# Layer epilogues by groups: GpSimd centres and squares, roots by parts, and the second half of the pair products first

## The chip, the cores and the metric

The kernel runs on one core of one Trainium2 chip. The metric is device time in microseconds (us), the median of several runs. Five engines work side by side: TensorE (PE, its weight loads listed as PEld), VectorE (DVE), ScalarE (ACT), GpSimd (POOL) and SyncE (SP, which here only issues DMAs). Each has its own instruction stream; they wait for one another through semaphores.

## The reference: four graph layers, each followed by a layer norm

There are 6250 nodes with 64 features and 200000 edges. Cut to what matters here:

```python
x = layernorm(x + relu((D^-1/2 A D^-1/2 x) @ W + b))             # layer 0
x = layernorm(x + relu(x @ U.T + segment_sum(x[src], dst) @ V.T))  # layer 1
x = layernorm(x + (concat([mean_agg(x), x]) @ W.T + b))            # layer 2
# layer 3: for each edge
h = relu(concat([x[src], x[dst]]) @ W1 + b1)
i = h @ W2 + b2
g = i * sigmoid(i @ Wg + bg)
x = layernorm(x + segment_sum(g, src) / max(count(src), 1))
# layernorm(x) = (x - mean) / sqrt(var + 1e-5), over the 64 features
```

## The kernel before, in words

The nodes lie in 49 tiles of 128 rows, padded to `NTP` = 50; `X`, `AGG` and `T1` are [128, 50, 64] fp32 in SBUF. Most passes over them go by groups of 8 tiles (512 elements a partition): `EG` = 7 groups, the last with 2 tiles (128 elements).

The program first sorts the edges, then builds the dense adjacency matrix in DRAM, then runs layers 0 to 2. Each of these streams the adjacency rows in (SP's queue) and multiplies them on TensorE into an accumulator that fills seven PSUM banks. Behind that comes the **epilogue** of the layer: VectorE copies the accumulator to `AGG`, TensorE transposes it (and `X`) group by group, ScalarE copies the transposes to SBUF, TensorE multiplies by the weights, and VectorE adds the residual (`out`), takes the mean, centres, squares and sums the squares (`centre`), all of a group before the next one. After the last group it takes `variance` of all 50 tiles in one instruction, ScalarE takes one root, VectorE one reciprocal (`inverse_root`), and then it normalises group 0 and splits it into three bf16 parts (`split`) that the next layer's accumulation starts from.

After layer 2 all groups are normalised, then transposed and multiplied by the two halves of W1 (`turn_pairs`, `pair_product`). The products with the first half (A rows) stay in SBUF, split in three bf16 parts in `x3`; those with the second half (B rows) go to `AGG` and from there to a table in DRAM, `b_table`.

Layer 3 then goes over 440 *items*, each a part of one of 391 groups of 512 edges (padded to 392 groups). For each group GpSimd issues four indirect DMAs (gathers) that fetch the B rows of its 4 x 128 edges into one of `RING` = 8 slots (`gather_group`). TensorE, ScalarE and VectorE work an item through `hidden`, `interact`, `gate`, `gated` and `sum_edges`. The sequencer of GpSimd tells the others that a group has landed:

```python
if not first or s >= GLAG:                 # GLAG = 2: the group two back
    e.wait_ge(b_landed[(s - GLAG) % RING], 16 * G * (rnd + (s >= GLAG)))
    e.sem_inc(groups_landed, 1)
```

The start of the gathers hangs on `table_out` (the whole of `b_table` stored); the start of the items on `a_split` (the A rows split, `total` cleared). At the end VectorE divides `total` by the counts, adds, centres, squares and normalises, at full width, and SP stores the output in two parts.

All order is written out by hand: each engine's stream is what the code says, and the waits are on the numbers in `mark`. Line numbers in the rows below are those of this kernel: L800 to L805 `out`, L729 to L733 `centre`, L740 the reciprocal, L743 `normalise`, L717 to L721 `split`, L1444 the accumulation, L1512 the pair products, L976 the copy of the gather's indices, L994 the gathers.

## Time and profile before

| | us |
|---|---|
| median of 3 runs | 4379.18 (4379.10 to 4385.17) |
| the profiled execution, its own time | 4377.39 |
| its span in the trace | 4375.7 |
| PE busy | 3589.0 (82%) |
| DVE busy | 2414.6 (55%) |
| ACT busy | 1724.7 (39%) |
| POOL busy | 1570.6 (36%) |

The span is the profiled execution from its first to its last instruction; 1.7 us lie around it. The busy time of an engine is a mean over stages that have little in common: POOL is idle for most of the first 2329 us and busy without a break in the last stage. Times in the rows count from the start of the span.

### The profile page before, as it was taken

What the parts mean: (1) busy time and instruction counts of PE and PEld (TensorE: products, weight loads), DVE (VectorE), ACT (ScalarE), POOL (GpSimd) and SP (SyncE); (2) the same over time, 40 slices, a digit from 0 to 9 for tenths busy, and PEclk for the clock granted to TensorE, in tenths of its full rate; (3) what the DMA queues carried; (4) which work ended last, traced back from release to release, by engine and by line L of the source; (5) the groups of instructions that cost most, each with busy time, mean ns of one, the idle gap of its engine ahead of it and who ended that gap; (6) DMA issues with size and microseconds to landing.
All of it is one profiled execution on the core that took longest, in us unless ns stands there. A gap on an engine that the chain in (4) does not pass through costs nothing.

```text
span 4375.7 us, 127467 instructions
## 1 busy us (share of the span) xinstructions
PE 3589.0 (82%) x39375; PEld 2793.3 (64%) x39376; DVE 2414.6 (55%) x6572; ACT 1724.7 (39%) x3798; POOL 1570.6 (36%) x1730
## 2 busy tenths in 40 slices
PE   5784247777777798898996999889999999999886
PEld 2342123333333598897985877777877777878775
DVE  8988879999999702305024434433434343343344
ACT  5773037777777400001002434333333333343332
POOL 2000010000000000000005777777777777777773
PEclk9896579998888899999996979998889888788996
DMA  1000012222222597796962222222222222222222
GB/s 43 3 4 1 19 61 88 88 97 94 88 88 103 194 349 293 276 349 229 343 244 49 57 51 59 56 55 55 56 54 57 54 56 56 54 57 55 56 55 37
DMA packets 186859, 446.38 MB, mean 102 GB/s; under 512 B 52907, under 2 KB 115379, under 8 KB 180271
## 3 DMA queue, kind: packets, MB, share of 16 engines
q1 hardware_dynamic: 133263, 388.80, 25.6%
q0 software_dynamic: 51328, 54.71, 6.1%
q10 hardware_dynamic: 2208, 2.10, 0.2%
q8 instruction: 34, 0.56, 0.1%
q14 instruction: 26, 0.21, 0.0%
HBM read 357.45 MB, written 87.99 MB: 102 GB/s over the span
## 4 chain that ended last, share of the span: by engine, by line
PE 50%; DVE 19%; issue 10%; DMA 9%; POOL 7%; ACT 3%; ACTq 1%; POOLq 1%; DVEq 1%; SPq 0%; PEldq 0%
PE ps L1444 11%; DVE x L509 9%; PE ps L1419 8%; PE ps L1539 8%; PE ps L1529 7%; PE ps L1551 7%; PE ps L1526 6%; POOL x L994 6%; DMA rows<-adjacency 4%; DMA x<-b_table,gidx 4%; DVE rows L707 4%; ACT stage L1193 1%; PE ps L1326 1%; ACT ps L1174 1%; POOLq L988 1%
## 5 line engine op out<-in xcount | busy, mean ns | idle before, releaser
L994 POOL DMA_INDIRECT x<-b_table,gidx x1568 | 1500.1, 957 | 464.0 <-issue 375.7
L1419 PE MATMUL ps<-rows 128*128 128x448 bf16 x2272 | 650.3, 425 | 222.1 <-DVE rows L707 96.6
L1444 PE MATMUL ps<-x,rows 128*128 x22050 | 684.5, 194 | 57.3 <-DVEq L757 29.4
L1444 PEld LDWEIGHTS ps<-x,rows 128*128 128x128 bf16 x22050 | 667.2, 98 | 75.3 <-issue 65.9
L707 DVE TENSOR_SCALAR rows<-iota_c,x 128x448 bf16<-128x448 bf16 x2272 | 711.0, 408 | 2.3 <-PE ps L1419 2.3
L855 DVE TENSOR_TENSOR x<-x,ps 128x256 f32<-128x256 f32 x440 | 185.3, 421 | 945.2 <-ACT x L1260 942.3
L1419 PEld LDWEIGHTS ps<-rows 128*128 128x128 bf16 x2272 | 332.1, 146 | 540.0 <-issue 422.0
L1539 PE MATMUL ps<-w2cat,x 65*128 65x128 f32 x3520 | 575.4, 313 | 0.0
L1529 PEld LDWEIGHTS ps<-ident,x 128*64 128x64 f32 x3520 | 486.9, 157 | 106.6 <-issue 42.9
L1551 PE MATMUL ps<-x 128*128 128x65 f32 x3520 | 503.7, 291 | 49.2 <-DVE x L855 48.4
L1539 PEld LDWEIGHTS ps<-w2cat,x 65*128 65x128 f32 x3520 | 485.0, 214 | 89.2 <-issue 87.7
L1529 PE MATMUL ps<-ident,x 128*64 128x128 f32 x3520 | 539.6, 305 | 0.0
L1551 PEld LDWEIGHTS ps<-x 128*128 128x128 f32 x3520 | 486.2, 214 | 60.1 <-DVE x L855 59.5
L1526 PE MATMUL ps<-x 128*64 128x512 bf16 x1320 | 424.7, 436 | 115.8 <-issue 83.0
L1254 ACT ACTIVATE x<-ps,b1col 64x512 f32<-64x512 f32 x440 | 299.2, 680 | 486.9 <-PE ps L1529 484.5
L1247 ACT ACTIVATE x<-x 128x256 f32 x442 | 184.0, 416 | 735.7 <-POOLq L982 561.8
L1193 ACT ACTIVATE stage<-ps 128x448 bf16<-128x448 f32 x700 | 386.1, 552 | 217.1 <-PE ps L1419 207.5
L509 DVE TENSOR_TENSOR x<-x 128x512 f32<-128x512 f32 (+1 forms) x516 | 401.6, 835 | 5.6
L847 DVE TENSOR_SCALAR x<-iota_f,stage 128x128 f32<-128x128 f32 x1760 | 398.3, 304 | 0.1
L1174 ACT ACTIVATE ps<-zero_col 128x448 f32<-128x448 f32 x707 | 390.8, 562 | 0.1
L780 DVE MEMSET AGG<- 128x64 f32 x3 | 0.3, 112 | 613.3 <-PEq L1450 613.3
L965 POOL DMA_INDIRECT T<-key_rows,item_group x4 | 3.8, 942 | 917.7 <-DVE x L760 916.8
(280 smaller groups left out, 2490.3 us busy)
## 6 DMA issues: line engine op xcount, KB each, us to landing
rows<-adjacency SPq DMA_DIRECT2D x150, 800.0 KB, 6.2
rows<-adjacency SPq DMA_DIRECT2D x150, 768.0 KB, 6.0
adjacency<-stage SPq DMA_DIRECT2D x50, 1568.0 KB, 5.1
x<-src_rows SPq DMA_DIRECT2D x440, 128.0 KB
x<-b_table,gidx POOLq DMA_INDIRECT x1568
key_rows<-x ACTq DMA_DIRECT2D x1, 1024.0 KB, 4.1
pair_rows<-x ACTq DMA_DIRECT2D x1, 1024.0 KB, 7.3
pair_rows<-x SPq DMA_DIRECT2D x1, 1024.0 KB, 5.4
```

Of the source, the lines that this page charges most:

```text
L509: ins = e.tensor_tensor(view(b, high, down), view(a, 0, down), view(a, 1, down), op)
L707: ins = e.tensor_scalar(hot_dst[:, k, :], iota_c[:], rel_col[:, bass.ds(i0 + k, 1)], digit_col[:, bass.ds(i0 + k, 1)], ALU.is_equal, ALU.mult)
L847: ins = e.tensor_scalar(OS[:, s, j, :], iota_f[:], src_items[:, bass.ds(G * i + j, 1)], None, ALU.is_equal)
L994: e.indirect_dma_start(out=BGT[:, s, j, :], out_offset=None, in_=b_table, in_offset=bass.IndirectOffsetOnAxis(ap=gidx[:, s * G + j:s * G + ...
L1174: e.activation(ps[:, bank, 0:WIN], repeat(zero_col[:], WIN), ACT.Copy).then_inc(evicted, 1)
L1193: e.activation(stage[:, h, v * WIN:(v + 1) * WIN], ps[:, v % RINGW, 0:WIN], ACT.Copy).then_inc(strip_out, 1)
L1419: e.matmul(psf[:, bass.ds(at_bank, WIN)], hot_src[:, k // HOTS, :, k % HOTS], hot_dst[:, k % HOTS, :], start=False, stop=False, skip_group ...
L1444: ins = e.matmul(acc_ps[:, t, :], rows[:, h, c:c + P], x3[:, bass.ds(2 * pr + h // 2, 1), k * D:(k + 1) * D] .rearrange("p a f -> p (a f)" ...
L1526: e.matmul(ps[0:D, u, :], AT[:, s, k * D:(k + 1) * D], OT[:, u, :], start=(k == 0), stop=False, skip_group_check=True)
L1529: ins = e.matmul(ps[0:D, u, j * P:(j + 1) * P], BT[:, s, j * D:(j + 1) * D], ident[:], start=False, stop=(j == G - 1), skip_group_check=True)
L1539: ins = e.matmul(ps[:, 2 + u, j * P:(j + 1) * P], H[0:D + 1, u, j * P:(j + 1) * P], w2cat[:], start=True, stop=True)
L1551: ins = e.matmul(ps[:, 4 + u, 0:D + 1], OS[:, s, j, :], MG[:, u, j, :], start=(j == 0), stop=(j == G - 1))
```

## The change

Six edits, all in what stands between the big stages and in the last one's gathers:

1. `centre` is cut in three. VectorE sums the rows and scales the mean (`sum_rows`); GpSimd adds the mean and squares, in two `tensor_tensor` a group; VectorE sums the squares of the group two back (`sum_squares`).
2. `variance`, root and reciprocal go by two parts, tiles 0 to 31 and 32 to 49 (`ROOT`), in layers 0, 1 and the last norm, and by groups in layer 2. The second part's sums stand behind the split of group 0.
3. In layer 2 the pair products start from centred, not normalised rows; each row of the product is multiplied by its inverse root as it leaves PSUM. B products stand in the layer's own loop (`b_products`, `b_rows`), A products behind it. The bias of layer 2 is added to `X` into `T1` while the accumulation runs.
4. `b_table` is stored in three parts, each as soon as its groups are there. Clearing `total` and scaling `X` by the inverse roots goes to ScalarE (50 small instructions); the A rows are split group by group.
5. `GLAG` is 1 instead of 2, and the wait for the group before stands between the second and the third gather of a group instead of ahead of the first.
6. The last norm goes by groups, with GpSimd's share as in 1, and the output is cut at tile 32 instead of 25.

```diff
+            def sum_rows(layer, g):
+                t0, t1 = group_tiles(g)
+                mean = stat[:, 0, t0:t1]
+                e.wait_ge(dve, q.n)
+                q.link(e.tensor_reduce(mean, X[:, t0:t1, :], AX_X, ALU.add))
+                q.mark(f"mean{layer}_{g}", e.tensor_scalar(mean, mean, -1.0 / D, None, ALU.mult))
+            def sum_squares(layer, g):
+                t0, t1 = group_tiles(g)
+                e.wait_ge(centred, 2 * (layer * EG + g) + 2)
+                q.done(e.tensor_reduce(stat[:, 1, t0:t1], T1[:, t0:t1, :], AX_X, ALU.add))
...
-                    centre(t0, t1)
-                mark[f"var{layer}"] = variance()
+                    sum_rows(layer, g)
+                    if layer < 2:
+                        if g >= 2:
+                            sum_squares(layer, g - 2)
+                        if g == EG - 2:
+                            variance(f"var{layer}_0", 0, ROOT[1])
+                    else:
+                        if g >= 2:
+                            sum_squares(2, g - 2)
+                            variance(f"var2_{g - 2}", *group_tiles(g - 2))
+                        if g >= 3:
+                            b_rows(g - 3)
+            for g in (EG - 2, EG - 1):
+                sum_squares(2, g)
+                variance(f"var2_{g}", *group_tiles(g))
+                b_rows(g - 2)
+            b_rows(EG - 2)
+            b_rows(EG - 1)
...
+                def b_rows(g):
+                    t0, t1 = group_tiles(g)
+                    inverse_root(5 + g, t0, t1)
+                    e.wait_ge(pair_product, g + 1)
+                    q.mark(f"p_{g}", e.tensor_tensor(
+                        AGG[:, t0:t1, :], ps[:, 6 + g % 2, 0:(t1 - t0) * D].rearrange("p (t f) -> p t f", f=D),
+                        over_f(stat[:, 0, t0:t1]), ALU.mult))
...
+            def centre(layer, g):
+                n = layer * EG + g
+                t0, t1 = 8 * g, min(8 * g + 8, NTP)
+                xs = X[:, t0:t1, :]
+                e.wait_ge(dve, mark[f"mean{layer}_{g}"])
+                e.tensor_tensor(xs, xs, over_f(stat[:, 0, t0:t1]), ALU.add).then_inc(centred, 1)
+                e.wait_ge(centred, 2 * n + 1)
+                e.tensor_tensor(T1[:, t0:t1, :], xs, xs, ALU.mult).then_inc(centred, 1)
...
-                if not first or s >= GLAG:
-                    e.wait_ge(b_landed[(s - GLAG) % RING], 16 * G * (rnd + (s >= GLAG)))
-                    e.sem_inc(groups_landed, 1)
...
                 for j in range(G):
+                    if j == 2 and (not first or s >= GLAG):
+                        e.wait_ge(b_landed[(s - GLAG) % RING], 16 * G * (rnd + (s >= GLAG)))
+                        e.sem_inc(groups_landed, 1)
...
+                def b_products(g):
+                    e.wait_ge(pairT_copied, g + 1)
+                    if g >= 2:
+                        e.wait_ge(dve, mark[f"p_{g - 2}"])
+                    else:
+                        e.wait_ge(item_copied, ITEM_BLOCKS)
+                    pair_products(g, 6 + g % 2, 1)
```

The first place is VectorE's epilogue of layer 0, from the first group on. Before (L729 to L733 are `centre`):

```order
L800 TENSOR_TENSOR T<-ps,bias 128x512 [waits product]
L802 SCALAR_TENSOR_TENSOR X<-T,X 128x512 [waits dve]
L729 TENSOR_REDUCE stat<-X 128x8 [waits dve]
L730 TENSOR_SCALAR stat<-stat 128x8 [waits dve]
L731 TENSOR_TENSOR X<-X,stat 128x512 [waits dve]
L732 TENSOR_TENSOR T<-X 128x512 [waits dve]
L733 TENSOR_REDUCE stat<-T 128x8 [waits dve]
```

The same engine and layer in the changed kernel, the third group (g = 2), where L744 sums the squares of group 0:

```order
L826 TENSOR_TENSOR T<-ps,bias 128x512 [waits product]
L828 SCALAR_TENSOR_TENSOR X<-T,X 128x512 [waits dve]
L738 TENSOR_REDUCE stat<-X 128x8 [waits dve]
L739 TENSOR_SCALAR stat<-stat 128x8 [waits dve]
L744 TENSOR_REDUCE stat<-T 128x8 [waits centred]
```

Two of a group's seven instructions have gone from VectorE, and the last sum waits for GpSimd's second instruction of the group two back.

The second place is the end of layer 2's epilogue on VectorE in the changed kernel, from the small last group on; L814 is the multiplication in `b_rows`:

```order
L833 TENSOR_TENSOR X<-ps,T 128x128 [waits product]
L738 TENSOR_REDUCE stat<-X 128x2 [waits dve]
L739 TENSOR_SCALAR stat<-stat 128x2 [waits dve]
L744 TENSOR_REDUCE stat<-T 128x8 [waits centred]
L748 TENSOR_SCALAR stat<-stat 128x8 [waits dve]
L752 RECIPROCAL stat<-stat 128x8 [waits root_ready]
L814 TENSOR_TENSOR AGG<-ps,stat 128x512 [waits pair_product,dve]
L744 TENSOR_REDUCE stat<-T 128x8 [waits centred]
L748 TENSOR_SCALAR stat<-stat 128x8 [waits dve]
L752 RECIPROCAL stat<-stat 128x8 [waits root_ready]
L814 TENSOR_TENSOR AGG<-ps,stat 128x512 [waits pair_product,dve]
```

The first L814 here is `b_rows(3)` of the loop's g = 6, the second is `b_rows(3)` again, from g = 5 of the loop behind it: the group's rows are written twice.

The third place is GpSimd's loop of gathers, one group. Before (L988 loads a number that the group's wait for a free slot needs; `b_landed1` belongs to the group two back):

```order
L988 ISA [waits b_landed1]
L988 TENSOR_LOAD last_use
L988 ISA x2
L994 DMA x<-b_table,gidx 128x64 [waits b_copied]
L994 DMA x<-b_table,gidx 128x64 x3
```

And one group of the changed kernel, where `b_landed1` belongs to the group just before:

```order
L1043 ISA
L1043 TENSOR_LOAD last_use
L1043 ISA x2
L1052 DMA x<-b_table,gidx 128x64 [waits b_copied]
L1052 DMA x<-b_table,gidx 128x64
L1052 DMA x<-b_table,gidx 128x64 [waits b_landed1]
L1052 DMA x<-b_table,gidx 128x64
```

The wait for a landing has moved from the head of a group to its middle, and from the group two back to the one before: two gathers stand between the awaited group's last one and the wait, where there were four.

## Rows read from the trace of the kernel before

**Rows 1.** Page, costliest groups: line, engine, op, count | busy, mean ns | idle before.
```profile
L994 POOL DMA_INDIRECT x<-b_table,gidx x1568 | 1500.1, 957 | 464.0 <-issue 375.7
```

**Rows 2.** Timeline of POOL, 2264 to 2385 us: start, us, op, count [idle before <-releaser].
```profile
2329.20 1.93 POOL L976 COPY gidx<-dst_pad 128x16 int32<-128x16 int32 x2 [815.26 <-DMA b_table<-AGG]
2331.28 5.31 POOL L994 DMA_INDIRECT x<-b_table,gidx  x1
2336.89 5.08 POOL L994 DMA_INDIRECT x<-b_table,gidx  x1 [0.30 <-issue]
```

**Rows 3.** Timeline of DVE, 1724 to 1775 us (epilogue of layer 0).
```profile
1730.63 0.69 DVE L800 TENSOR_TENSOR T<-ps,bias 128x512 f32<-128x512 f32 x1 [0.58 <-PE ps L1489]
...
1732.08 0.69 DVE L729 TENSOR_REDUCE stat<-X 128x8 f32<-128x512 f32 x1
...
1733.01 0.69 DVE L731 TENSOR_TENSOR X<-X,stat 128x512 f32<-128x512 f32 x1
...
1757.93 0.29 DVE L800 TENSOR_TENSOR T<-ps,bias 128x128 f32<-128x128 f32 x1
...
1761.94 0.47 DVE L740 RECIPROCAL stat<-stat 128x50 f32<-128x50 f32 x1 [1.67 <-ACT stat L1227]
1762.44 0.69 DVE L743 TENSOR_TENSOR X<-X,stat 128x512 f32<-128x512 f32 x1
...
1765.54 0.43 DVE L721 CAST x<-AGG 128x512 bf16<-128x512 f32 x1
```

**Rows 4.** Timeline of PE: accumulation starts again, layers 1 and 2.
```profile
1766.31 8.87 PE L1444 MATMUL ps<-x,rows 128*128 x248 [15.14 <-DVEq L757]
...
2035.41 8.77 PE L1444 MATMUL ps<-x,rows 128*128 x236 [14.23 <-DVEq L757]
```

**Rows 5.** Timeline of PE, 1996 to 2044 us: transposes of two groups of layer 1.
```profile
2004.16 0.60 PE L1463 MATMUL ps<-ident,AGG 128*128 128x128 f32 x4
...
2006.82 0.60 PE L1463 MATMUL ps<-ident,AGG 128*128 128x128 f32 x4
```

**Rows 6.** Groups by line and form on POOL.
```profile
L927 POOL TENSOR_SCALAR_AFFINE_SELECT stage<-stage 3x492 f32<-3x492 f32 x2 | 1.1, 585 | 0.1
```

**Rows 7.** Timeline of DVE and PE, 2264 to 2385 us (layer 2's epilogue and the pairs).
```profile
2275.22 0.69 DVE L800 TENSOR_TENSOR T<-ps,bias 128x512 f32<-128x512 f32 x1 [2.52 <-PE ps L1491]
...
2331.11 3.49 DVE L718 TENSOR_TENSOR AGG<-T,x 128x3200 f32<-128x3200 f32 x1
2334.64 1.83 DVE L719 CAST x<-AGG 128x3200 bf16<-128x3200 f32 x1
...
2316.84 1.95 PE L1512 MATMUL ps<-wb,xT 128*128 128x128 f32 x16
```

**Rows 8.** Chain that ended last, by pieces: start, us, what (2324 us, then layer 3).
```profile
2324.66 4.49 DMA b_table<-AGG
...
2368.58 3.79 DMA x<-b_table,gidx
...
2913.65 2.27 DMA x<-b_table,gidx
...
4163.63 2.43 DMA x<-b_table,gidx
4166.24 0.28 POOLq L988
```

**Rows 9.** Timeline of POOL, 4150 to 4180 us.
```profile
4169.95 1.08 POOL L994 DMA_INDIRECT x<-b_table,gidx  x1 [0.30 <-issue]
```

**Rows 10.** Windows of layer 3: us, busy (count) of PE, PEld, DVE, ACT, POOL, PEclk, DMA.
```profile
4280.00:4300.00 20.00, 20.00 (x82) 16.56 (x82) 5.47 (x21) 5.20 (x12) 15.27 (x18) 0.50 0.19 46
```

**Rows 11.** Timeline of DVE, 4310 to 4380 us (the last norm).
```profile
4341.59 3.49 DVE L889 TENSOR_TENSOR AGG<-stage,scale 128x3200 f32<-128x3200 f32 x1
...
4363.96 3.69 DVE L743 TENSOR_TENSOR X<-X,stat 128x1600 f32<-128x1600 f32 x2
```

More of the change, by code:

```diff
@@ L86 @@
 HALF_RING = RING // 2
-GLAG = 2
+GLAG = 1
 GR = -(-GROUPS // RING) * RING
@@ L712, in _, with split @@
             e.wait_ge(evicted, levels * WINDOWS + RINGW)
-            def split(src, t0, t1):
-                v, rest = src[:, t0:t1, :], AGG[:, t0:t1, :]
+            def split(src, t0, t1, rest):
+                v = src[:, t0:t1, :]
                 q.link(e.tensor_copy(x3[:, t0:t1, 0:D], v))
@@ L778, in _ @@
                                                             None, ALU.subtract))
+                if layer == 2:
+                    q.link(e.tensor_tensor(T1[:], X[:], bias[:, 1, :].unsqueeze(1).to_broadcast([P, NTP, D]), ALU.add))
                 e.wait_ge(agg_ready, layer + 1)
@@ L795, in _ @@
                     xs = X[:, t0:t1, :]
-                    if layer == 1:
+                    if layer == 0:
+                        q.link(e.tensor_tensor(T1[:, t0:t1, :], o,
+                                               bias[:, 0, :].unsqueeze(1).to_broadcast([P, t1 - t0, D]), ALU.add))
+                        q.done(e.scalar_tensor_tensor(out=xs, in0=T1[:, t0:t1, :], scalar=0.0, in1=xs,
+                                                      op0=ALU.max, op1=ALU.add))
+                    elif layer == 1:
@@ L797, in _ @@
                         q.done(e.scalar_tensor_tensor(out=xs, in0=o, scalar=0.0, in1=xs, op0=ALU.max, op1=ALU.add))
                     else:
-                        bb = bias[:, layer // 2, :].unsqueeze(1).to_broadcast([P, t1 - t0, D])
-                        q.link(e.tensor_tensor(T1[:, t0:t1, :], o, bb, ALU.add))
-                        if layer == 0:
-                            q.done(e.scalar_tensor_tensor(out=xs, in0=T1[:, t0:t1, :], scalar=0.0, in1=xs,
-                                                          op0=ALU.max, op1=ALU.add))
-                        else:
-                            q.done(e.tensor_tensor(xs, T1[:, t0:t1, :], xs, ALU.add))
@@ L823, in _ @@
-            e.wait_ge(dve, q.n)
-            mark["b_rows"] = q.n
-            e.wait_ge(table_out, 32)
-            split(T1, 0, NTP)
-            q.done(e.memset(total, 0.0))
+                        q.done(e.tensor_tensor(xs, o, T1[:, t0:t1, :], ALU.add))
+                    mark[f"out{layer}_{g}"] = q.n
+                    sum_rows(layer, g)
[10 more added lines that the diff above has]
+                            b_rows(g - 3)
@@ L828, in _ @@
+            for g in (EG - 2, EG - 1):
[4 more added lines that the diff above has]
+            b_rows(EG - 1)
             q.done(e.memset(MG[:, :, :, D:D + 1], 1.0))
             q.done(e.memset(H[D:D + 1, :, :], 1.0))
-            e.wait_ge(dve, q.n)
+            for g in range(EG):
+                t0, t1 = group_tiles(g)
+                e.wait_ge(pair_product, EG + g + 1)
+                q.mark(f"a_{g}", e.tensor_tensor(
+                    T1[:, t0:t1, :], ps[:, g % 4, 0:(t1 - t0) * D].rearrange("p (t f) -> p t f", f=D),
+                    over_f(stat[:, 0, t0:t1]), ALU.mult))
+                e.wait_ge(dve, q.n)
+                split(T1, t0, t1, rest_a[:, g % 2, 0:t1 - t0, :])
@@ L968, in _ @@
                 ).then_inc(items_gathered, 16)
-            e.wait_ge(table_out, 32)
+            def centre(layer, g):
[6 more added lines that the diff above has]
+                e.tensor_tensor(T1[:, t0:t1, :], xs, xs, ALU.mult).then_inc(centred, 1)
+            for layer in range(3):
+                for g in range(EG):
+                    centre(layer, g)
+            e.wait_ge(table_out, 48)
             def keep_ids(g, half):
@@ L979, in gather_group @@
                 g = RING * rnd + s
-                if not first or s >= GLAG:
-                    e.wait_ge(b_landed[(s - GLAG) % RING], 16 * G * (rnd + (s >= GLAG)))
-                    e.sem_inc(groups_landed, 1)
-                if s == GLAG - 1 and not first:
+                if s == GLAG and not first:
                     keep_ids(g - s + HALF_RING, 1)
-                if s == HALF_RING + GLAG - 1:
+                if s == HALF_RING + GLAG:
                     keep_ids(g - s + RING, 0)
@@ L1008, in _ @@
                 e.sem_inc(groups_landed, 1)
+            for g in range(EG):
+                centre(3, g)
         @block.sync
@@ L1213, in _, with pair_copy, root @@
                     turn_items(b)
+                def pair_copy(g):
+                    w = (min(8 * g + 8, NTP) - 8 * g) * D
+                    e.wait_ge(pair_turned, g + 1)
+                    e.activation(pairT[:, g, 0:w], ps[:, 3, 0:w], ACT.Copy).then_inc(pairT_copied, 1)
+                def root(name, t0, t1):
+                    e.wait_ge(dve, mark[name])
+                    e.activation(stat[:, 2, t0:t1], stat[:, 1, t0:t1], ACT.Sqrt).then_inc(root_ready, 1)
                 for g in range(EG):
@@ L1277, in _ @@
             gate(ITEMS - 1, (ITEMS - 1) % 2, False)
-            e.wait_ge(dve, mark["var3"])
-            e.activation(stat[:, 2, :], stat[:, 1, :], ACT.Sqrt).then_inc(root_ready, 1)
+            for half in range(2):
+                root(f"var3_{half}", ROOT[half], ROOT[half + 1])
         @block.tensor
```

172 lines of the change are left out of this document (99 added, 73 removed).

## The prediction

> **What bounds the kernel now.** I read the page first. GpSimd has one group of 1568 gathers: 957 ns each, with 464.0 us of gaps put down to issue [rows 1]. Busy time and gaps together are 1964 us, and the timeline of POOL shows them back to back from 2331.28 on, one each 1.25 us (0.94 busy, 0.30 issue). So layer 3 ends when the gathers end, and they end as much earlier as they begin earlier: TensorE, at half clock near the end (0.50 for the twenty microseconds of [rows 10]), only has some items in arrears behind the last gather.
>
> Ahead of that stand three epilogues. In each one VectorE works almost without a gap, and the next stage waits for it: TensorE's accumulation of layers 1 and 2 had stood idle for 15.14 and 14.23 us until VectorE's split of group 0 [rows 4]; the gathers waited for the table's store, which waited for VectorE's copies of the pair products. So each microsecond taken off VectorE there goes one to one into the end, as long as TensorE, ScalarE or GpSimd doesn't become the slower one. The last norm is VectorE alone.
>
> All sums below are made against the profiled execution, 4377.4 us (span 4375.7); the median of the runs is 1.8 us higher.
>
> **GpSimd's price.** No row has a `tensor_tensor` on GpSimd. The nearest is a select with one fp32 input and one output, 585 ns for 492 columns, 1.19 ns a column [rows 6]: 0.6 us for 512 columns is the low end. With two inputs fetched in turn it is twice that, which I take: 1.2 us. The high end is three passes, 1.8 us. A group costs GpSimd two of them, 2.4 us (1.2 to 3.6), against 1.4 us for VectorE.
>
> The Trainium skill (GPSIMD Engine Reference, section 3.1) gives 4497 ns for a two-input fp32 add of 2048 elements; my estimate from that page is 1.1 us for 512. No run here shows it yet; with it the sum would change by less than a microsecond.
>
> **Layer 0: -9.5 us.** From the first group's `out` at 1730.63 to the restart of TensorE at 1766.31 are 35.7 us. What is left to VectorE for a group are the bias, the residual, the sum and the scaled mean, 1730.63 to 1733.01: 2.38 [rows 3]. From the third group on a sum of squares comes in, 0.72. So 2 x 2.38 + 4 x 3.10 + 0.2 (first variance) + 1.2 (small group, by its 0.29 us instructions) + 0.72 (one more sum) = 19.3. Reciprocal to restart is 4.4 now (1761.94 to 1766.31) and stays; the root and the clearing of the accumulator, which kept the reciprocal waiting 1.67 us [rows 3], are hidden, because the root stands ahead of the clearing. That is 23.7, or -12.0. But the residual has two SBUF inputs, and so have GpSimd's adds and multiplications. 0.69 + 2.4 us of such work a group leaves no room in 3.1; I give 2.5 us back. Range -12 to -5.
>
> What shows that they collide: the first two gathers took 5.31 and 5.08 us instead of 0.94 [rows 2]. The first began inside a `tensor_tensor` of 3.49 us and ended 0.1 us behind the cast of 1.83 us that followed [rows 7]; the index copies, 1.93 us for two small ones, ended with the cast just ahead of that `tensor_tensor` [rows 2, 7]. So a VectorE instruction of either kind holds GpSimd off for its whole length. The Trainium skill (SBUF — State Buffer, "Who interferes with whom") has it as an exclusive lock on a port pair, taken by casts in their fast mode, and for reads by instructions with two SBUF inputs; the trace agrees. It adds that the loser waits on either side, which no row here can show; by it, the give-backs here and in the last norm stay, and without it they would be nil.
>
> **Layer 1: -8.5 us.** VectorE would need 1.65 a group and 0.72 for the squares, 2.4, less than TensorE, whose groups follow each other every 2.66 us [rows 5]. So TensorE paces it: product 0 done at 2004.16, product 5 at 2017.5. Then 2.38 + 0.2 + 0.85 + 0.72 + 4.4 gives 2026.0 against 2035.41: -9.4. GpSimd at 2.4 plus handoff is just as fast and has two groups of slack; 0.9 given back. Range -10 to -4.
>
> **Layer 2 to the first gather: -22 us.** TensorE's step grows: 8 transposes and 16 passes in 2.66 are 0.11 each (the pair products, 16 in 1.95, say the same [rows 7]); 4 transposes and 8 passes more make 4.0. VectorE's step is 1.65 (`out`, sums) + 0.92 (squares, variance) + 0.94 (reciprocal, multiplication) = 3.5. So TensorE paces: from the first product at 2275.2 [rows 7] the sixth is there at 2275.2 + 2.7 + 3.5 + 4.0 + 4.0 + 3.3 = 2292.7. Behind it VectorE has 3.5, then 2.7 for the small group, then 1.86 with the doubled `b_rows(3)` (0.9 of it wasted), 1.46 and 0.94: B rows of group 5 at 2303.2. The store took 4.49 us from issue to landing [rows 8]: 2307.7. The index copies then take 0.5 to 2.1 (2.08 now, 2329.20 to 2331.28): first gather at 2309.0 against 2331.28. The bias addition lies under the 270 us of accumulation [rows 4]. ScalarE's clearing and its 50 small ones lie under the split of the A rows: at VectorE's 3.49 for a full-width pass and 0.29 for 128 columns 18 us, against 23; were they longer, the items would start later, which the ring absorbs (below). SP's queue has nothing between the stores. Range -25 (VectorE alone paces) to -14 (a microsecond more a group).
>
> **Start of the gathers: -4.5 us.** Now the first two lose 8.5 us to the wide split. In the changed kernel the split runs by groups for some 23 us, from about 2304.5, and so beside some 15 gathers; each can meet a `tensor_tensor` of 0.69 and a cast of 0.43. On average, half an instruction times its share of the time, that is 0.2 us each, 3 us; at worst 1.1 us each, 17. I take 4 lost. Range -8.5 to +8. The items begin when the split ends, about 20 us behind the first gather (17.8 now); the ring holds eight groups, 40 us of gathers, so that costs nothing.
>
> **GLAG and the moved wait: +8 us.** Here the change speaks against itself. The chain shows a last gather of a group that starts at 4163.63 and lands 2.43 later, at 4166.06, and GpSimd's sequencer at the head of the group two further on at 4166.24; that group's first gather runs at 4169.95 [rows 8, 9]. So the sequencer is three gathers ahead of its engine, the announcement already comes at the landing, and the lag of two costs nothing: there is nothing to win by 1. What is lost is slack. The third gather of the next group is due 3 x 1.25 = 3.75 us behind the awaited one's start. A landing takes 2.4. For the restart behind a wait I take the 0.30 us of issue that lie between any two gathers; the index copy began 0.05 behind the table's landing (2324.66 + 4.49 = 2329.15, then 2329.20) and the gather 0.15 behind the copies [rows 2, 8]. So most groups pass with 1.0 to spare. But of 69 landings in the chain of layer 3, from 2.27 to 3.79 us, seven take 3.50 or more [rows 8]; with 0.30 each of these is 0.1 to 0.4 late, 0.2 on average, and 391 groups have some 40: 8 us. Range 0 to +30, the high end if the restart costs 0.8.
>
> **Last norm: +3 us; arrears: -3 us.** From 4341.59 to 4363.96 VectorE runs seven full-width passes of 3.49 [rows 11]. GpSimd takes two, 7.0; cutting the other passes in groups costs 1.1 each for four (7 x 0.72 against 3.5, less the small group), 4.5, and 1.2 for the means: -1.3. But both its divisions and its additions have two SBUF inputs, 1.4 + 2.4 us of colliding work in 3.1 a group: about 0.7 to 1.1 a group lost. Together +3, range -1.3 to +8. TensorE's arrears behind the last gather (25 us here, with the half clock just before it [rows 10]) depend on where the slow stretches fall: -3, range -10 to +3.
>
> **Sum**: -9.5 - 8.5 - 22 - 4.5 + 8 + 3 - 3 = -36.5: 4377.4 - 36.5 = 4340.9. I say 4341, 0.87% below the median.
>
> **The rivals.**
> - *GpSimd paces* (0.17). At 1.8 us an instruction, or held off by VectorE's, a group takes it 3.6 to 4.3 us in layers 0, 1 and the norm. Layer 0 then wins 5, layer 1 4, layer 2 20, the norm loses 8: 4377.4 - 29 - 4.5 + 8 + 8 - 3 = 4357. For it: the collisions of [rows 2, 7]. Against: the sum of squares looks two groups back.
> - *The moved wait never bites, and no arrears* (0.13). Late landings are covered, and the slow clock ends early: the 8 go and 5 more come: 4328. For it: three of the seven late landings are under 3.75.
> - *The moved wait bites in every group* (0.05). If the restart behind the wait costs 1.45 us and not 0.30, the median landing (2.4) misses 3.75 by 0.1, and the late ones by 1.4: 36 + 55 = 91 us against the 44 that the rest wins: 4424, slower. It decides from about 1.2 us on. Against it: the 0.05 and 0.15 of [rows 2, 8].
> - *Nothing much is left* (0.05): GpSimd at its high price and the split fully in the gathers' way, 17 lost instead of 4: 4357 + 13 = 4370, at the edge of no change.
> - The forecast holds 0.60, with 4330 to 4353.
>
> **How the numbers follow.** The range takes in the second and third case and leaves out the last two: 4322 to 4362. A measurement here can tell about 0.2%, 8.8 us, from no change. Faster: 0.60 + 0.17 + 0.13 and half of the last, 0.92; same 0.03, slower 0.05.
>
> **What the changed profile would show.** TensorE's accumulation of layer 1 restarts 26 us behind the first `out` of layer 0 (35.7 before), that of layer 2 23 us behind (31 before). GpSimd's `tensor_tensor` rows have a mean near 1.2 us; near 1.8, the second case. The first gather follows layer 2's first `out` by 34 us (56 before). The gathers' idle time grows by some 8 us with a DMA as releaser, and the mean of one stays near 957 ns. The last norm takes a little longer than before. Wrong would be: gathers with waits in each group, or a sum of squares that waits each time for GpSimd.

## The result, and the profile after it

The changed kernel took 4366.9 us (median of 9 runs, 4357.8 to 4373.3), the kernel before beside it 4379.1 (9 runs, 4373.2 to 4394.9). The ratio of the two is 0.997, 95% interval 0.9956 to 0.9983: 12 us faster. The prediction said 4341, 38 us faster, with a range from 4322 to 4362; the measured time lies outside it.

The profiled execution took 4357.8 us, its span 4356.1, against 4377.4 and 4375.7: 19.6 us less. It is the shortest of the nine executions, 9 us under their median, so its stages show a little more gain than the median does. I read it stage by stage.

**Layer 0.** Timelines of DVE, of POOL and of PE, changed kernel: VectorE's first groups, GpSimd's first group, then TensorE's restart.

```profile
1731.45 0.69 DVE L826 TENSOR_TENSOR T<-ps,bias 128x512 f32<-128x512 f32 x1 [0.58 <-PE ps L1597]
1732.18 0.69 DVE L828 SCALAR_TENSOR_TENSOR X<-T,X 128x512 f32<-128x512 f32 x1
...
1737.03 1.04 DVE L828 SCALAR_TENSOR_TENSOR X<-T,X 128x512 f32<-128x512 f32 x1
...
1740.22 1.57 DVE L828 SCALAR_TENSOR_TENSOR X<-T,X 128x512 f32<-128x512 f32 x1
```

```profile
1733.89 1.04 POOL L1021 TENSOR_TENSOR X<-X,stat 128x512 f32<-128x512 f32 x1 [219.02 <-DVE stat L739]
1735.00 1.37 POOL L1023 TENSOR_TENSOR T<-X 128x512 f32<-128x512 f32 x1
```

```profile
1757.79 4.44 PE L1522 MATMUL ps<-x,rows 128*128 x77 [11.38 <-DVEq L770]
...
2018.19 4.01 PE L1522 MATMUL ps<-x,rows 128*128 x69 [8.54 <-DVEq L770]
```

From 1731.45 to 1757.79 are 26.3 us, against 35.7 [rows 3, 4]. The two engines do hold each other off, both ways: GpSimd's instructions took 1.04 us in most groups and 1.37 where VectorE's residual ran just then (L1023 at 1735.00, the residual of 1734.42 to 1735.47), and the residual with its two SBUF inputs (L828) took 1.04 to 1.57 from the second full group on, instead of 0.69.

**Layer 1.** The second row of PE above ends a stretch that begins with the first `out` here (timeline of DVE):

```profile
1996.60 0.69 DVE L831 SCALAR_TENSOR_TENSOR X<-ps,X 128x512 f32<-128x512 f32 x1 [1.58 <-PE ps L1599]
...
1999.26 0.69 DVE L831 SCALAR_TENSOR_TENSOR X<-ps,X 128x512 f32<-128x512 f32 x1 [1.04 <-PE ps L1599]
```

21.6 us to 2018.19; VectorE waits for TensorE's product in each group, every 2.66 us, as foreseen.

**Layer 2 up to the gathers.** Timelines of DVE, SP and POOL:

```profile
2259.48 0.69 DVE L833 TENSOR_TENSOR X<-ps,T 128x512 f32<-128x512 f32 x1 [2.86 <-PE ps L1599]
...
2265.63 0.69 DVE L833 TENSOR_TENSOR X<-ps,T 128x512 f32<-128x512 f32 x1 [1.87 <-PE ps L1599]
...
2269.62 0.69 DVE L833 TENSOR_TENSOR X<-ps,T 128x512 f32<-128x512 f32 x1 [1.22 <-PE ps L1599]
...
2287.17 0.69 DVE L814 TENSOR_TENSOR AGG<-ps,stat 128x512 f32<-128x512 f32 x1 [0.97 <-PE ps L1570]
...
2287.97 0.29 DVE L814 TENSOR_TENSOR AGG<-ps,stat 128x128 f32<-128x128 f32 x1
```

```profile
2284.89 7.74 SPq L1155 DMA_DIRECT2D b_table<-AGG  x3
```

```profile
2294.74 0.38 POOL L1034 COPY gidx<-dst_pad 128x16 int32<-128x16 int32 x2 [12.36 <-DMA b_table<-AGG]
2295.78 1.28 POOL L1052 DMA_INDIRECT x<-b_table,gidx  x1 [0.65 <-POOL gidx L1034]
2297.36 0.94 POOL L1052 DMA_INDIRECT x<-b_table,gidx  x1 [0.31 <-issue]
```

The step of TensorE is 3.99 us (2265.63 to 2269.62; the forecast had 4.0). The first gather comes 36.3 us behind the first `out`, against 56.1 [rows 2, 7]. SP issues the three stores between 2284.89 and 2292.63 us. The second keeps its queue until 2289.40, so that the last is issued at 2289.45, 1.2 us behind VectorE's last B rows (2288.26), and it lands 5.24 us later by the chain; from those rows to the index copies are 6.5 us. And the first gather takes 1.28 us and the second 0.94, where the wide split had made them 5.31 and 5.08 [rows 2].

**The gathers.** The page's row of them, which answers to [rows 1]:

```profile
L1052 POOL DMA_INDIRECT x<-b_table,gidx x1568 | 1490.0, 950 | 499.7 <-issue 398.2
```

Busy time fell by 10.1 us, the gaps grew by 35.7. First and last start stand in the view of one source line (count: duration ns min/median/max, first and last start), here for the kernel before and then for the changed one:

```profile
L994 POOL DMA_INDIRECT x<-b_table,gidx x1568: 940/944/5309, 2331.3 to 4314.8; - x196
```

```profile
L1052 POOL DMA_INDIRECT x<-b_table,gidx x1568: 938/944/1277, 2295.8 to 4305.4; - x196
```

So the loop of gathers, from the first start to the last, took 1983.5 us before and takes 2009.6 now: 26 us more, although its start no longer loses 8 us. It begins 35.5 us earlier and ends only 9.4 earlier. Where they go is seen in any stretch. Timeline of POOL, then the chain of waits, both of the changed kernel:

```profile
2317.33 0.94 POOL L1052 DMA_INDIRECT x<-b_table,gidx  x1 [0.30 <-issue]
2319.06 0.94 POOL L1052 DMA_INDIRECT x<-b_table,gidx  x1 [0.78 <-DMA x<-b_table,gidx]
```

```profile
2314.84 3.45 DMA x<-b_table,gidx
```

The awaited group's last gather starts at 2314.84 and lands at 2318.29; the third gather of the next group, due at 2318.58, starts at 2319.06, 0.77 us behind the landing. Over the whole loop I counted in the trace 87 of 391 groups whose third gather has a gap of more than 0.35 us ahead of it, and each of them starts 0.77 to 0.79 us behind the landing. The excess over a gap of 0.31 is 31.5 us ahead of third gathers and 3.2 ahead of second ones; the kernel before has none at either place.

**The end.** Timeline of DVE in the last norm, and the windows around the last gather (columns as in [rows 10]):

```profile
4319.10 0.69 DVE L928 TENSOR_TENSOR AGG<-stage,scale 128x512 f32<-128x512 f32 x1
...
4331.93 1.17 DVE L928 TENSOR_TENSOR AGG<-stage,scale 128x512 f32<-128x512 f32 x1
4333.12 1.41 DVE L929 TENSOR_TENSOR X<-X,AGG 128x512 f32<-128x512 f32 x1
...
4347.18 1.36 DVE L755 TENSOR_TENSOR X<-X,stat 128x1152 f32<-128x1152 f32 x1
```

```profile
4280.00:4300.00 20.00, 20.00 (x135) 16.89 (x134) 7.67 (x29) 7.84 (x20) 14.97 (x18) 0.87 0.27 50
4300.00:4312.00 12.00, 10.86 (x82) 9.01 (x81) 5.32 (x21) 4.88 (x13) 4.66 (x5) 1.00 0.38 16
```

The norm's passes take 29.4 us (4319.10 to 4348.54) against 26.1 [rows 11]: a group costs 4.04 us, and its two instructions with two SBUF inputs 1.17 and 1.41 instead of 0.69. TensorE's arrears, from the last gather's start to the sums' completion, were 13 us here and 26 before: the granted clock was 0.87 and 1.00 around the last gather, where it had been 0.50, the lower of its two levels (1.2 GHz).

### The profile page after: what moved, and what is told of

Read it like the earlier page. It is cut to its first block, busy times and chain, and to the rows that moved or that the text cites. A ratio compares the mean times of both kernels' runs of the same rounds, so it can differ in the third digit from the quotient of the medians.

```text
span 4356.1 us, 127600 instructions
## 1 busy us (share of the span) xinstructions
PE 3581.7 (82%) x39375; PEld 2783.7 (64%) x39376; DVE 2389.9 (55%) x6594; ACT 1737.6 (40%) x3858; POOL 1616.1 (37%) x1786
## 4 chain that ended last, share of the span: by engine, by line
PE 35%; DVE 18%; issue 15%; DMA 13%; POOL 12%; POOLq 3%; ACT 2%; ACTq 1%; DVEq 1%; SPq 0%; PEldq 0%
PE ps L1522 12%; POOL x L1052 11%; DVE x L516 9%; DMA x<-b_table,gidx 9%; PE ps L1497 8%; DVE rows L714 4%; DMA rows<-adjacency 4%; PE ps L1640 3%; PE ps L1630 3%; PE ps L1652 3%; PE ps L1627 3%; POOLq L1043 3%; ACT stage L1252 1%; PE ps L1404 1%; ACT ps L1233 1%
## 5 line engine op out<-in xcount | busy, mean ns | idle before, releaser
L714 DVE TENSOR_SCALAR rows<-iota_c,x 128x448 bf16<-128x448 bf16 x2272 | 737.3, 594 | 2.1 <-PE ps L1497 2.1
```

The lines of the kernel that those rows point to most:

```text
L714: ins = e.tensor_scalar(hot_dst[:, k, :], iota_c[:], rel_col[:, bass.ds(i0 + k, 1)], digit_col[:, bass.ds(i0 + k, 1)], ALU.is_equal, ALU.mult)
```

## The experiments

Theory S: the gain is there, and layer 3 gives most of it back, because a gather behind a wait starts 0.77 us behind the landing and two gathers are too little slack for that. Against it stand the A split and ScalarE's work beside the gathers (R), the lag of one as such (D), and TensorE close behind the gathers, which would take back at the end what they win (P).

A plain fact about the runs first. The kernel before took 4381 us in the set with e1b, e2b, e3b and e5, as in the first measurement, and 5237 to 5287 us in the three other sets. There the mean granted clock of the profiled runs was 0.77 to 0.79 instead of 0.870 to 0.893, and the gathers no longer set the pace of layer 3: they stood behind ScalarE's copies, as the rows of e0 show. I call these the low clock. The sets also ran on different chips: the three at the low clock on the machine's chips 0, 12 and 12, the one with e1b on chip 14; for the first measurement the chip is not on record. Times are compared within a set only, or as ratios.

**e0, e1, e2, e3** ran together, at the low clock. e0 is the changed kernel itself. e1 puts the wait back:

```diff
-GLAG = 1
+GLAG = 2
...
+                if not first or s >= GLAG:
+                    e.wait_ge(b_landed[(s - GLAG) % RING], 16 * G * (rnd + (s >= GLAG)))
+                    e.sem_inc(groups_landed, 1)
-                if s == GLAG and not first:
+                if s == GLAG - 1 and not first:
...
-                    if j == 2 and (not first or s >= GLAG):
-                        e.wait_ge(b_landed[(s - GLAG) % RING], 16 * G * (rnd + (s >= GLAG)))
-                        e.sem_inc(groups_landed, 1)
```

e2 makes the reverse of this edit in the kernel before, and nothing else of the change:

```diff
-GLAG = 2
+GLAG = 1
...
-                if not first or s >= GLAG:
-                    e.wait_ge(b_landed[(s - GLAG) % RING], 16 * G * (rnd + (s >= GLAG)))
-                    e.sem_inc(groups_landed, 1)
...
+                    if j == 2 and (not first or s >= GLAG):
+                        e.wait_ge(b_landed[(s - GLAG) % RING], 16 * G * (rnd + (s >= GLAG)))
+                        e.sem_inc(groups_landed, 1)
```

e3 is the changed kernel with

```diff
-                    if j == 2 and (not first or s >= GLAG):
+                    if j == 3 and (not first or s >= GLAG):
```

Expected of e0: 

> The changed kernel itself, unchanged, as the measure for the three that run beside it. Both theories: its median near 4367 us, 0.997 of the kernel before; the loop of gathers (start of the first to start of the last) near 2010 us; some 85 of 390 groups with a gap of over 0.35 us ahead of their third gather.

Expected of e1: 

> The changed kernel with the gathers' wait as it was: lag of two groups, at the head of a group. Theory S (lost slack: behind a landing that comes later than 3.0 us the third gather starts 0.77 us behind that landing, and nothing makes it up): the gathers' loop takes 1975 to 1985 us instead of 2010, gaps with a DMA as releaser go from some 240 to under 20; the time falls by 22 (if TensorE's arrears at the end grow back to 25 us from 13) to 35 us: 4332 to 4345. Rival R (the gathers are slower for what else changed beside them: the A split by groups, ScalarE's 50 small scalings, the clearing): the loop stays near 2010 and the time near 4367.

Expected of e2: 

> The kernel before with the lag of one and the moved wait alone. Theory S: the loop grows from 1983 to 2010 to 2020 us, and the time by 22 to 35 us: 4401 to 4414, slower. Rival R: nothing changes, 4379.

Expected of e3: 

> The changed kernel with the lag of one, but the wait ahead of the fourth gather of a group and not of the third. Theory S: the fourth is due 5.0 us behind the start of the awaited one; less the restart of 0.77 that allows landings up to 4.2 us, of which there are under 1 in 100: the loop takes 1975 to 1988 us, the time 4332 to 4347, the same as with the wait at the head. Rival D (it is the lag of one itself, a wait on a group that has just been issued, wherever it stands, that breaks the sequencer's run ahead): the loop stays near 2010 and the time near 4367.

Measured, as ratio to the kernel before (5287 us): e0 0.9896 (0.9858 to 0.9933), e1 0.9939 (0.9915 to 0.9962), e2 1.0009 (0.9988 to 1.003), e3 0.9899 (0.9866 to 0.9932). None of the expected times came, since the gathers were not the bound. Windows of layer 3 in e0, and what its gathers waited for (us, times):

```profile
2400.00:5100.00 2700.00, 2205.20 (x11165) 1792.97 (x11164) 727.17 (x2885) 705.30 (x1652) 1417.44 (x1564) 0.69 0.17 38
```

```profile
  ACT x L1325: 837.7, 201
```

A granted clock of 0.69 (the same window view of the first profile of the changed kernel has 0.87) is a mean over the two levels, and the gathers stand 838 us behind ScalarE's copies, that is, behind a ring that is not emptied fast enough. The traces tell the theories apart all the same: counted as above, the excess in the gaps ahead of third gathers was 33.4 us in e0, 24.3 in e2, and 0.0 in e1 and e3. Late starts come with the wait at that place and go with it; here nothing hung on them.

**e1b, e2b, e3b, e5** ran together, at the first clock. The first three are the same kernels again. e5 is e1 with the doubled `b_rows(3)` taken out and the last norm on VectorE alone:

```diff
-            for g in (EG - 2, EG - 1):
-                sum_squares(2, g)
-                variance(f"var2_{g}", *group_tiles(g))
-                b_rows(g - 2)
+            sum_squares(2, EG - 2)
+            variance(f"var2_{EG - 2}", *group_tiles(EG - 2))
+            sum_squares(2, EG - 1)
+            variance(f"var2_{EG - 1}", *group_tiles(EG - 1))
+            b_rows(EG - 3)
...
+            q.link(e.tensor_tensor(AGG[:], total[:, :, 0:D], over_f(scale[:, 2, :]), ALU.mult))
+            q.link(e.tensor_tensor(X[:], X[:], AGG[:], ALU.add))
+            q.link(e.tensor_reduce(stat[:, 0, :], X[:], AX_X, ALU.add))
+            q.link(e.tensor_scalar(stat[:, 0, :], stat[:, 0, :], -1.0 / D, None, ALU.mult))
+            q.link(e.tensor_tensor(X[:], X[:], over_f(stat[:, 0, :]), ALU.add))
+            q.link(e.tensor_tensor(T1[:], X[:], X[:], ALU.mult))
+            q.link(e.tensor_reduce(stat[:, 1, :], T1[:], AX_X, ALU.add))
```

Expected of e1b: 

> The kernel of e1 again, hoped for at the clock of the first profiles (mean 0.875 over the run; the first four runs had 0.77, with TensorE as the bound of layer 3 and gathers that waited for ScalarE's copies). At that clock theory S: the gathers' loop takes 1975 to 1985 us, gaps ahead of the third gather all 0.31, and the time falls to 4332 to 4345. Rival R (something else beside the gathers): loop near 2010, time near 4367. Rival P (TensorE stands close behind the gathers, so that what they win it loses again in arrears at the end): the loop as in S, but the arrears grow by as much and the time stays above 4355. If the clock is 0.77 again, both loop and time are TensorE's: no difference from the changed kernel by more than 0.3%.

Expected of e2b: 

> The kernel of e2 again. At the clock of the first profiles theory S: the loop grows from 1983 to 2010 to 2020 us, the time to 4401 to 4414. Rival R: 4379. Rival P: the loop grows as in S, but part of it is taken back at the end: 4385 to 4400. At 0.77: no difference.

Expected of e3b: 

> The kernel of e3 again. At the clock of the first profiles theory S: as e1b, loop 1975 to 1988 us and 4332 to 4347. Rival D (the lag of one itself costs): near 2010 and 4367. The traces of e0 and e3 speak for S already: excess over 0.31 us in the gaps ahead of the third gather 33 us there and none here.

Expected of e5: 

> The kernel of e1 with group 3's B rows made once and the last norm on VectorE alone at full width, as before the change. Theory S: 1 us from the first (the first gather starts 35.3 us behind layer 2's first out, not 36.3), 3 us from the second (from the first wide pass to VectorE's last instruction 26 us, not 29): 4 us less than e1b. Rival: the norm by groups had hidden its output behind work, so that the tail grows by what the norm wins: the same as e1b.

Measured beside 4381.2 us of the kernel before:

| | us | ratio (95%) | loop of gathers |
|---|---|---|---|
| changed kernel (first measurement, beside 4379.1) | 4366.9 | 0.997 (0.9956 to 0.9983) | 2009.6 |
| e1b, wait at the head | 4337.2 | 0.9898 (0.988 to 0.9917) | 1976.5 |
| e2b, moved wait in the kernel before | 4421.3 | 1.0095 (1.0074 to 1.0117) | 2023.4 |
| e3b, wait ahead of the fourth | 4337.5 | 0.9898 (0.9878 to 0.9919) | 1976.1 |
| e5, once and wide | 4331.0 | 0.9893 (0.9872 to 0.9913) | 1974.7 |

The loops are read from one row of the source line's view each, e1b, e2b and e3b in this order:

```profile
L1052 POOL DMA_INDIRECT x<-b_table,gidx x1568: 938/944/1141, 2302.7 to 4279.2; - x196
```

```profile
L994 POOL DMA_INDIRECT x<-b_table,gidx x1568: 938/944/5313, 2344.7 to 4368.1; - x196
```

```profile
L1052 POOL DMA_INDIRECT x<-b_table,gidx x1568: 938/944/1276, 2308.8 to 4284.9; - x196
```

Edit 5 alone costs 40 us in the kernel before, in the time (4421.3 less 4381.2) and in the loop (2023.4 less 1983.5), and 33 us of loop in the changed one. e1b and e3b lie in their expected ranges; e2b lies above its own (2010 to 2020 and 4401 to 4414). The kernel before was not profiled in this set, so loops are compared across sets: that e2b's 40 and 40 agree is in part chance, for its arrears were 17 us instead of 26, and it took 13 us longer to its first gather, through stretches that edit 5 does not touch. R falls: with everything else of the change in place the loop is 7 us shorter than before. D falls: a lag of one with three gathers of slack costs nothing. P holds for the smaller part: e1b's arrears were 21 us against 13 in the changed kernel, so 8 of the 33 us came back at the end there, but e3b's and e5's were 15 with the same short loop. By the medians' ratios the wait costs 0.72% in the changed kernel (0.997 less 0.9898), 31 us. One reading of mine was wrong: I had expected gaps put down to a DMA to vanish in e1b. They did not (64.6 us, 212 times), but each is 0.30 long, the ordinary gap, only filed under the DMA. The length of a gap tells a stall, its releaser's name does not.

In e5, timeline of DVE, the wide norm:

```profile
4290.90 3.49 DVE L927 TENSOR_TENSOR AGG<-stage,scale 128x3200 f32<-128x3200 f32 x1
...
4313.35 3.56 DVE L755 TENSOR_TENSOR X<-X,stat 128x2048 f32<-128x2048 f32 x2
```

26.0 us, 3.4 less than by groups, of which the output's end takes 1.0 back (8.6 us behind VectorE's last instruction, 7.6 in the changed kernel). The single `b_rows(3)` brought the first gather from 36.3 to 35.0 us behind the first `out`. Those are 3.7 us by the rows; the measured 6.1 between e5 and e1b agrees with that, within what four runs each can tell. The runs alone don't separate the two kernels (ratios 0.9898 and 0.9893, with intervals that overlap). e5 beats both the kernel before, by 50 us, and the changed one.

**e0b, e4, e6, e8** ran together, at the low clock. e0b is the changed kernel again. e4 moves its wait ahead of the second gather:

```diff
-                    if j == 2 and (not first or s >= GLAG):
+                    if j == 1 and (not first or s >= GLAG):
```

e6 is e1 with GpSimd's two instructions given back to VectorE:

```diff
-                q.mark(f"mean{layer}_{g}", e.tensor_scalar(mean, mean, -1.0 / D, None, ALU.mult))
+                q.link(e.tensor_scalar(mean, mean, -1.0 / D, None, ALU.mult))
+                xs = X[:, t0:t1, :]
+                q.mark(f"cen{layer}_{g}", e.tensor_tensor(xs, xs, over_f(mean), ALU.add))
+                e.wait_ge(dve, q.n)
+                q.done(e.tensor_tensor(T1[:, t0:t1, :], xs, xs, ALU.mult))
```

e8 is e5 with layer 0's biased product written back to PSUM, so that the residual has one SBUF input:

```diff
-                        q.link(e.tensor_tensor(T1[:, t0:t1, :], o,
+                        q.link(e.tensor_tensor(o, o,
...
-                        q.done(e.scalar_tensor_tensor(out=xs, in0=T1[:, t0:t1, :], scalar=0.0, in1=xs,
+                        q.done(e.scalar_tensor_tensor(out=xs, in0=o, scalar=0.0, in1=xs,
```

Expected of e0b: 

> The changed kernel itself beside the three below. At the clock of the first profiles 4362 to 4372 us, the loop of gathers near 2010; that is 25 to 33 us above e1b.

Expected of e4: 

> The changed kernel with the wait ahead of the second gather of a group. It is due 2.5 us behind the start of the awaited one, whose landing takes 2.65 us in the mean: every group stalls. If a restart behind a landing costs 0.77 us whatever the place (theory S): 2.65 + 0.77 - 2.5 = 0.92 us a group, 390 groups, 360 us: loop near 2340, time 4670 to 4700 at the clock of the first profiles. If it is 0.30 and the rest of the loss has another cause: 0.45 a group, 175 us, time 4500 to 4530.

Expected of e6: 

> The kernel of e1 with centring and squaring back on VectorE, by groups as the rest; GpSimd's share alone is undone. Theory G (what GpSimd takes over is worth its 1.4 us a group less what the two engines hold each other off): layer 0 +4.5 us (8.8 less the 4.1 that the residuals lose now), layer 1 +7 (VectorE 3.8 a group against TensorE's 2.66), layer 2 +5 (4.9 against 4.0), norm +5: 20 to 24 us above e1b, 4357 to 4361. Rival (the pipeline by groups is what wins, and GpSimd's share adds nothing to speak of): under 5 us, 4342 at most.

Expected of e8: 

> The kernel of e5, in which layer 0's bias addition writes back to PSUM, so that the residual (L828 of the changed kernel) reads one operand from PSUM and one from SBUF and not two from SBUF. Theory L (a VectorE instruction with two SBUF inputs and GpSimd's tensor_tensor hold each other off, and only that made the residual 1.04 to 1.57 us): it takes 0.69 to 0.75 in each group, from layer 0's first out to TensorE's restart 22.5 to 23 us and not 26.3: 3 to 4 us less than e5. Rival (any VectorE work beside GpSimd's is slowed, or reading PSUM costs as much): the same as e5.

Measured beside 5248.2 us: e0b 0.9886 (0.9847 to 0.9924), e6 0.9952 (0.9927 to 0.9977), e8 0.9875 (0.9826 to 0.9924), and e4, one run, 5078.4 us. The times don't decide; the rows of the epilogues, which the clock of layer 3 doesn't touch, do. Timelines of DVE and PE in e8:

```profile
1739.67 0.70 DVE L826 TENSOR_TENSOR ps<-ps,bias 128x512 f32<-128x512 f32 x1 [1.50 <-PE ps L1590]
...
1747.79 0.69 DVE L828 SCALAR_TENSOR_TENSOR X<-ps,X 128x512 f32<-128x512 f32 x1
```

```profile
1762.10 20.50 PE L1515 MATMUL ps<-x,rows 128*128 x588 [9.86 <-DVEq L770]
```

The residual is at 0.69 in every full group, and TensorE restarts 22.4 us behind the first `out` instead of 26.3. So it was the second SBUF input that met GpSimd, and it cost 3.9 us. In e6, timelines of DVE and PE:

```profile
1738.19 0.69 DVE L830 TENSOR_TENSOR T<-ps,bias 128x512 f32<-128x512 f32 x1 [1.38 <-PE ps L1585]
...
2009.42 0.69 DVE L835 SCALAR_TENSOR_TENSOR X<-ps,X 128x512 f32<-128x512 f32 x1 [1.58 <-PE ps L1587]
```

```profile
1770.18 9.98 PE L1510 MATMUL ps<-x,rows 128*128 x276 [13.40 <-DVEq L774]
...
2036.77 19.40 PE L1510 MATMUL ps<-x,rows 128*128 x588 [12.49 <-DVEq L774]
```

32.0 us in layer 0 (26.3 with GpSimd) and 27.3 in layer 1 (21.6); layer 2's first gather was 40.4 us behind (36.3), the norm with the output 4.0 us longer. GpSimd's share is worth 5.7 + 5.8 + 4.1 + 4.0 = 19.6 us, read from rows. The rest of what the three epilogues win, 38.6 less 15.6 = 23 us, comes from the other edits together (work by groups, roots by parts, B products ahead of the norm), which no run takes apart. The rival, that GpSimd adds nothing, falls by the rows; at the low clock the time shows little of it (e6 0.9952 against e1's 0.9939).

**e4b, e6b, e8b** repeat e4, e6 and e8; the clock was low once more.

Expected of e4b: 

> The kernel of e4 again. At the clock of the first profiles theory S: each start of a second gather 0.77 us behind the landing it waits for, 2.65 + 0.77 - 2.5 = 0.92 us more a group, loop near 2340, time 4670 to 4700; with a restart of 0.30: 4500 to 4530. At the low clock the first time of e4 (5078, 0.968 of the kernel before) speaks for a gain from a slower feed of items; if it was chance, it comes out at 0.985 to 0.992 as the others of that call.

Expected of e6b: 

> The kernel of e6 again. Its rows of the low clock gave 5 us in layer 0, 4 in layer 1, 4 in layer 2 and 4 in the norm above the changed kernel. At the clock of the first profiles 17 us above e1b: 4354, 0.9935 to 0.9945 of the kernel before. Rival (TensorE's arrears take a part of it back): 4345 to 4350.

Expected of e8b: 

> The kernel of e8 again. Its rows of the low clock show the residual at 0.69 us in each group and 22.4 us to TensorE's restart instead of 26.3. At the clock of the first profiles 4 us less than e5: 4327, 0.987 to 0.989 of the kernel before; the difference to e5 lies within what three rounds can tell.

Measured beside 5237.5 us: e4b 0.9687 (0.9657 to 0.9717), e6b 0.9955 (0.9932 to 0.9977), e8b 0.9883 (0.9856 to 0.991). Whether e8 is faster than e5 at the first clock was not measured; its 3.9 us stand in the rows alone. The expected 360 us of e4 could not show either. What its traces show is the floor: over all groups of e4b with a gap ahead of the second gather, none started less than 0.77 us behind its landing, as in the changed kernel (third gather) and in e2b. So the least cost is the same at two places and both clocks, which S asked for. The usual cost at the low clock is larger, with a median of 0.98 us in e4b and 1.24 in e0 (third gather), and why is not shown. And at the low clock e4's kernel is the fastest, in both sets.

## Why the prediction missed, step by step

The step that failed is "GLAG and the moved wait: +8 us". Its mechanism was right, late landings against a slack of 3.75 us, and its high end, "+30, the high end if the restart costs 0.8", was near. The size taken was wrong: 0.30 us for the restart, measured 0.77. With 0.77, landings of more than 2.98 us are late, not of more than 3.45; these were 87 groups and not some 40, and each lost 0.36 us on average and not 0.2. That is 32 us ahead of the third gathers; the loop as a whole lost 33 (2009.6 against e1b's 1976.5). The 40 groups had been scaled up from seven landings of 3.50 and more in a sample of 69. The sample was not what misled: over all 392 groups in the trace of the kernel before, 33 last gathers land later than 3.45 us, which comes to 11 us by the prediction's own rule, and 94 later than 2.98, which comes to 38. The rule with 0.77 in it would have given e2b's loss from rows that were there beforehand. In the profiled run the step is 25 us worse than forecast, and 10 of these came back in the arrears.

Why 0.30 looked right: neither row behind it was the restart of a gather. The index copy 0.05 us behind the table's landing is no gather. The gather "0.15 behind the copies" does not wait for the second of the two copies but for the first (the group's wait asks for one count of `gidx_ready`), and the first had ended 1.9 us earlier, at 2329.40: it was the second that ran beside VectorE's cast and stretched the pair to 1.93 us. The row of the changed kernel shows it without that cover: a pair of copies from 2294.74, a first gather at 2295.78, 0.65 behind the end of the second and 0.8 to 0.85 behind that of the first. In a row that merges two instructions, the releaser can be the one that is hidden.

The other steps, from the profiled run, and with the wait back:

| step | predicted | changed kernel | e1b |
|---|---|---|---|
| layer 0, first `out` to restart | -9.5 | -9.3 | -9.3 |
| layer 1, first `out` to restart | -8.5 | -9.5 | -9.5 |
| layer 2, first `out` to first gather | -22 | -19.8 | -19.8 |
| start of the gathers | -4.5 | in the loop's +26 | -7.0 (loop) |
| moved wait | +8 | +33 (2009.6 less 1976.5) | 0 |
| last norm with output | +3 | +2.8 | +2.8 |
| arrears | -3 | -13 | -5 |
| all other stretches | 0 | +3 | +10 |
| the profiled run as a whole | -36.5 | -19.6 | -37.3 |

- Layers 0 and 1 came out within a microsecond. GpSimd's instruction was taken at 1.2 us and took 1.04. The estimate from the figure of the Trainium skill (GPSIMD Engine Reference, section 3.1) was 1.1 us, and the trace agrees with it.
- The 2.5 us given back in layer 0 were 4.1 (six residuals of 7.5 us together instead of 4.1, the small one 1.0 instead of 0.3), and the rest took 22.4 us (e8) and not 23.7: two errors that cancel, so that the sum for layer 0 is closer than its terms. The Trainium skill (SBUF — State Buffer, "Who interferes with whom") has it that the loser waits on either side, and that a VectorE instruction with at most one SBUF input, outside the fast modes, does not collide; the 1.04 to 1.57 us of L828 and its 0.69 in e8 agree with both.
- Layer 2 lacks 2.2 us. TensorE's step was right; the sum took 4.49 us for the store, and from the last B rows to the index copies it was 6.5 (1.2 until SP had issued the second store, 5.24 for the last one to land).
- The split by groups hardly touched the gathers: 7.0 us came back in the loop and 4.5 were forecast.
- The arrears fell by 13 in the changed kernel's profiled run and by 5 to 11 in the later ones. Part of this is that stalled gathers leave TensorE time to catch up, which I argue from e2b (17 us) and the changed kernel (13), and which the runs don't prove, because the clock near the end also differs from run to run.

Without the moved wait the prediction's sum is 44.5 us under the kernel before; e1b measured 44.0 under it in its own set (4381.2 less 4337.2). Such closeness is partly luck. The row of all other stretches holds what no step names, the time ahead of layer 0's first `out` and the two accumulations; in e1b these took 10 us more than in the first profile of the kernel before, and in e2b, which has the old epilogues, 13 more. So these 10 us are not the change's doing, but the steps of e1b are read against a profile from another set and are not sure to the microsecond. Of the rivals, GpSimd as the pace maker and the split in the gathers' way did not show; the wait that never bites is what e1b is, 9 us from that rival's 4328; the wait that bites in every group needed 1.2 us and had 0.77. The forecast of "faster" held, with less than a third of the gain, and the time was missed because a bound that I had written down was given too little weight.

## What to carry to other kernels

Before a wait is moved nearer to what it waits for, count the slack in time as it will be, landing plus restart, and take the restart from a row in which the same kind of instruction really stood behind a semaphore; if there is none, it is the widest unknown of the sum. An announcement that came early enough already (here the sequencer was three gathers ahead) gained nothing from a shorter lag at the first clock and lost the cover; one gather more of slack, in e3b, gave all of it back. Work moved to GpSimd won 4 to 6 us in each epilogue here against the same groups on VectorE alone (e6), even beside instructions with two SBUF inputs; these took 3.9 us of it in layer 0, and one operand in PSUM gave them back. Cutting a wide pass into groups for GpSimd's sake is another matter: the last norm was 2.8 us slower for it.

## What the hardware showed that was not expected

- A gather on GpSimd's queue that stands behind a wait starts 0.77 us behind the landing at the earliest, against a gap of 0.30 between gathers that don't wait.
- The kernel before took 4381 us in one set of runs and 5237 to 5287 in others; what differs in the profiles is layer 3, with a granted clock of 0.69 there and 0.87 in the first one. TensorE was busy for 84% of the stretch of e0b below and for 92% of the same layer in the first profile. Which of the two is the cause, and what sets the level, the chip or something else, no run here shows.
- At that clock the kernel whose gathers wait most for landings (e4, e4b) is 2% faster than the changed one. Windows of layer 3, e0b and then e4b:

```profile
2400.00:4900.00 2500.00, 2095.03 (x10627) 1700.15 (x10627) 696.07 (x2757) 670.22 (x1575) 1348.96 (x1486) 0.69 0.18 39
```

```profile
2400.00:4900.00 2500.00, 2157.14 (x11108) 1757.55 (x11109) 729.07 (x2884) 698.08 (x1648) 1408.78 (x1549) 0.70 0.18 41
```

In the same 2500 us TensorE did 4.5% more instructions in e4b, with 62 us less idle time and 1.5% less for each. A more even feed is a guess; the cause stays open.
